# Causal attention on Trainium2: TensorE takes scores and values of two sets in turn, where it took one and one

## What is computed

```python
# second attention (called AG in the kernel): softmax, causal, 16 heads of 8
scores = jnp.einsum('bhqd,bhkd->bhqk', q, k) / np.sqrt(HD)
probs = jax.nn.softmax(jnp.where(causal, scores, -1e30), axis=-1)
out = jnp.einsum('bhqk,bhkd->bhqd', probs, v)
# last attention (AR): relu, causal, 16 heads of 8
att = jax.nn.relu(scores) * causal
att = att / (jnp.sum(att, axis=-1, keepdims=True) + 1e-09)
ctx = jnp.einsum('bhqk,bhkd->bhqd', att, v)
```

## Time and profile before

| | |
|---|---|
| median of 3 runs | 1069.61 us (1068.16 to 1070.17) |
| the profiled execution's own time | 1072.35 us |
| its span in the trace | 1070.2 us |
| mean granted TensorE clock | 0.937 of full speed |
| TensorE busy with matmuls | 959.2 us, 90% |
| VectorE, ScalarE, GpSimd busy | 543.8, 544.1, 148.1 us |

### The profile page before, as it was taken

One profiled execution on the slowest core, in us unless ns is written; L12 is line 12 of the kernel. 1 busy time (PEld: TensorE's weight loads), 2 busy tenths in 40 slices (PEclk: granted clock), 3 DMA queues, 4 the chain that ended last, 5 costly groups with the idle time before them and its releaser, 6 DMA issues.

```text
span 1070.2 us, 24001 instructions
## 1 busy us (share of the span) xinstructions
PE 959.2 (90%) x10552; PEld 444.5 (42%) x10552; DVE 543.8 (51%) x878; ACT 544.1 (51%) x767; POOL 148.1 (14%) x164
## 2 busy tenths in 40 slices
PE   7357878899999998997899798998999999999898
PEld 3245653333333334884333333443333333344343
DVE  4535544553333356565555444546666665424454
ACT  5114444589999965542745551227555554445121
POOL 2300110050100103101011040000223223004000
PEclk9689998999999999558999899999999999998999
DMA  9564310010000000000000017400000000000841
GB/s 306 159 148 103 95 45 2 0 41 2 2 2 2 2 2 1 4 4 2 0 1 0 1 39 155 113 14 0 2 2 2 2 2 2 0 1 32 162 111 54
DMA packets 18851, 43.23 MB, mean 40 GB/s; under 512 B 5360, under 2 KB 5808, under 8 KB 17200
## 3 DMA queue, kind: packets, MB, share of 16 engines
q1 hardware_dynamic: 18748, 41.71, 15.3%
HBM read 36.91 MB, written 4.55 MB: 39 GB/s over the span
## 4 chain that ended last, share of the span: by engine, by line
PE 72%; ACT 8%; DVE 8%; DMA 7%; SPq 3%; issue 2%; POOL 0%; DVEq 0%; POOLq 0%
PE ps L1588 72%; DMA stf<-aux 2%; ACT nrr L798 2%; ACT nrr L796 1%; DMA stf<-scr_w 1%; SPq L516 1%; SPq L591 1%; DVE mxq L1215 1%; ACT work L1043 1%; DMA scr_k<-work 1%; DMA scr_q<-work 1%; DMA hz<-aux 0%; DVE work L1542 0%; ACT nrr L785 0%; SPq L560 0%
## 5 line engine op out<-in xcount | busy, mean ns | idle before, releaser
L1588 PE MATMUL ps<-rq,stf 32*64 32x512 f32 (+4 forms) x4096 | 213.4, 469 | 3.0 <-ACT hz L946 1.6
L1588 PE MATMUL ps<-work,vbuf 64*32 64x96 f32 (+6 forms) x3712 | 197.0, 387 | 0.7 <-issue 0.5
L1588 PE MATMUL ps<-hz,wsb 128*128 128x512 f32 (+1 forms) x352 | 161.3, 620 | 4.0 <-ACT nsq L787 3.5
L1588 PEld LDWEIGHTS ps<-rq,stf 32*64 32x64 f32 x4096 | 102.3, 152 | 108.0 <-issue 80.3
L902 ACT ACTIVATE work<-ps 128x1024 f32<-128x1024 f32 x144 | 139.3, 1022 | 13.5 <-PE ps L1588 8.8
L1588 PEld LDWEIGHTS ps<-work,vbuf 64*32 64x32 f32 (+1 forms) x3712 | 72.8, 121 | 110.3 <-issue 63.0
L964 ACT ACTIVATE work<-ps 128x1024 f32<-128x1024 f32 x72 | 73.7, 1025 | 75.6 <-PE ps L1588 75.6
L1588 PE MATMUL ps<-work,wsb 128*128 128x512 f32 (+1 forms) x176 | 90.8, 610 | 10.6 <-DVE work L1495 7.8
L1588 PEld LDWEIGHTS ps<-hz,wsb 128*128 128x128 f32 (+1 forms) x352 | 62.2, 191 | 83.7 <-issue 70.3
L1012 ACT ACTIVATE work<-ps 128x512 f32<-128x512 f32 x48 | 28.7, 597 | 124.9 <-PE ps L1588 124.9
L1291 DVE TENSOR_TENSOR work<-work,csb 128x1024 f32<-128x1024 f32 (+1 forms) x40 | 41.6, 1040 | 95.9 <-ACT work L902 95.6
(11 more groups left out here) (195 smaller groups left out, 1182.1 us busy)
## 6 DMA issues: line engine op xcount, KB each, us to landing
stf<-scr_w SPq DMA_DIRECT2D x128, 128.0 KB, 4.0
wsb<-in_w SPq DMA_DIRECT2D x1, 3440.0 KB, 19.9
stf<-scr_q SPq DMA_DIRECT2D x12, 192.0 KB
rq<-in_rq SPq DMA_DIRECT2D x2, 1024.0 KB, 5.1
csb<-in_c SPq DMA_DIRECT2D x1, 2003.0 KB, 11.8
stf<-scr_k SPq DMA_DIRECT2D x9, 204.0 KB
scr_q<-work SPq DMA_DIRECT2D x6, 256.0 KB, 5.3
scr_k<-work SPq DMA_DIRECT2D x6, 256.0 KB, 5.4
```

The costliest lines, as they stand in the source:

```text
L1588: return nc.tensor.matmul(o, l, r, start=start, stop=stop, skip_group_check=True)
```

## The change

The order of the four calls on TensorE in `causal_attention` changes, for AG and AR. Nothing is added or removed: the matmuls, the waits inside `scores` and `values`, the buffers and the programs of the other engines are the same.

```diff
-                for n in range(NS * len(PASSES) + 2):
-                    if n < NS * len(PASSES):
-                        scores(n)
-                    if n >= 2:
-                        values(n - 2)
-                    if n == NS * len(PASSES):
-                        denominators(a, 0)
+                for n in range(0, NS * len(PASSES), 2):
+                    for ahead in (n, n + 1):
+                        scores(ahead)
+                    if n:
+                        for behind in (n - 2, n - 1):
+                            values(behind)
+                values(NS * len(PASSES) - 2)
+                denominators(a, 0)
+                values(NS * len(PASSES) - 1)
```

## The result

The changed kernel takes 1136.4 us (median of 4, 1132.3 to 1139.7) against 1069.9 for the kernel before in the same comparison: a ratio of 1.061, 95% interval 1.0555 to 1.0664, or 59 to 71 us slower. A second comparison with more runs gave 1134.0 (6 runs) against 1070.8 (11 runs), ratio 1.0585 (1.0544 to 1.0626), 58 to 67 us. The forecast was 1130.6 with a range of 1121 to 1146; the forecast difference of 61 us lies in both intervals.

A forecast was written before the change was run, and what follows sets the result against it. TensorE was taken to bound AG and AR; 0.89 us more a round, with start and tail, gave about +30.5 us in each, +61 on 1069.6, so 1130.6 us, range 1121 to 1146.

The forecast's parts named there:

- The ring: Each AG and AR round: first unit's reading, release, fourth unit, two values, next first unit: 5.14 us against 4.25.
- the fourth unit: Last score unit in a round of two sets; needs the first unit's PSUM banks, may start 2.2 us after it.
- the blocked unit: In TensorE's list, the last score unit of a round, awaiting its PSUM banks; values and all that follows wait behind it.
- the first rival: AG and AR: banks free in time, TensorE saves 0.25 us in each of 72 rounds, 1052 us; chance 0.05.
- The covers: Other waits in AG and AR (ScalarE's and VectorE's readings, `probs`, masks) fit within the 5.14 us round and add nothing.
- First and last round: In AG, first round 3.6 us, last readings 2.2 us, and a tail about 1.5 us longer from VectorE's late mask.
- the sum: AG from first Exp to last: 3.6 + 174.8 + 2.2 = 180.6 us; both attentions together +61 us.
- The rival with a falling clock: AG and AR: TensorE stands still about 1.2 us in each 5.14, so its clock falls; likelier 1147 us; chance 0.07.
- A change of kind: TensorE switching between scores and values in AG and AR: some 0.09 us each over going on with the same kind.

The follow-up runs named there:

- half Exp: ScalarE's Exp in AG over one head of each unit: changed kernel, AG from 187.0 to 170.4 us; kernel before, AG from 156.8 to 150.6.
- moved fourth unit: Changed kernel with the second unit of scores n + 1 issued after one set of values: 1124.8 us, ratio 1.0497.
- with the waits away: AG alone in twos, six one-bank PSUM places, both heads summed in one 64-row matmul: AG 138.5 us, against 148.8 in the old order.

## Why the prediction was right

**The ring.** It was forecast at 5.14 us and is 5.11. Reading 1.02 and release 0.05 came as read from the earlier trace rows; the fourth unit to the values 1.02 against 1.01 to 1.03; the start of scores to their reading 1.15 against 1.16. Values were put at 1.90 and took 1.85. The half Exp showed that the reading is on the ring once, and the moved fourth unit that the wait hangs on its place. In 36 of 36 rounds of AG and 35 of 36 of AR the fourth unit starts 0.05 us after the reading of the first ends.

**Who waits behind it.** Nothing passed the blocked unit from the third round on in either stage (the values start 1.02 us after it, rounds of 5.11 us throughout), and the first rival (1052) fell. The rule of the Trainium skill, "TensorE: Matmul & The Clock Gate" (Part 3, Packing small matmuls), that matmuls keep the order of the program, agrees with the trace so far as the wait goes. It doesn't agree within a set, where the odd unit's first passes start before the even unit's second ones.

**The covers.** The masks, the ring of `probs` and VectorE's units in AR cost nothing in the middle, as said: AG and AR have the same round to the hundredth, though their readers differ.

**First and last round.** From the first Exp to the last in AG 180.1 us were measured (229.4 to 409.5) against 180.6 by the sum. Two errors stand against each other in it: the ring too long by 0.03 us makes 1.1 us in 34 rounds, and in the last round the Exp of the fourth unit follows 2.75 us behind that of the first, not 2.2, since ScalarE reads the second and third unit in between. At the end the wait for VectorE's late mask is there, at its place:

```profile
410.02 0.69 DVE L1278 COPY nrr<-ps 128x512 f32<-128x512 f32 x1 [5.14 <-PE ps L1588]
410.63 1.82 DVE L1291 TENSOR_TENSOR work<-work,csb 128x512 f32<-128x512 f32 x2
...
411.46 1.06 PE L1588 MATMUL ps<-work,vbuf 128*32 128x512 f32 x8 [0.65 <-DVE work L1291]
```

The copy of the bank, the mask behind it, and TensorE's 0.65 us of idle time before the values of set 70. AG grew by 30.2 us and AR by 29.7, against 30.5 each: AR's values have no such wait at the end, and its sum was 0.8 us too high.

**The clock.** The rival with a falling clock fell: 1.00 in AR and 0.99 in AG as before. Its premise was too strong. Of the 1.2 us that TensorE was to stand still in each round, the third unit fills all but some 0.45 us, and the records show TensorE busy for 177.4 of 187.4 us in AG.

**Where the reasoning was off.** One reading and one size, neither of which the 61 us hung on.

The wait was said to cost nothing in the kernel before, and TensorE's work to be the whole of its 4.25 us. But the odd unit waited for ScalarE there too, in both attentions, and 0.14 us of each old round of AG hung on that reading. The 0.07 by which the odd unit is behind the even one was read as TensorE's own and is this wait. It stood in the numbers: the fourth unit "over 2 us" after the first, the release 2.2 us after it. The difference of 5.14 and 4.25 doesn't change by it, since 4.25 is measured.

A change of kind was put at 0.09 us and costs 0.15. I had compared the gap between kinds with the pass right behind a change, 0.45, and not with passes of one kind, 0.43. So the saving is 0.30 us a round and not 0.25; its share on the ring is why two sets of values took 1.85 and not 1.90. With both errors the first rival's gain was too small: with the waits away AG took 138.5 us in twos against 156.8 before, though that kernel leaves out half of the exponentials and adds up scores that belong apart.

The 61 us were of the right size within the stages (59.9). The ratios of the two comparisons come to 65 and 63 us, 2 to 4 above 61, with 61 inside both intervals; that excess, open as said above, is no part of the sum.

## What to carry to other kernels

Before units of one kind are grouped, count the buffers that stand between producer and consumer: four units in a row through three places put a producer behind a reader of its own group, and everything that follows in the producer's list waits as well. The price can be read from the kernel before: add up the ring (read, release, last unit, what stands behind it, first unit until it can be read) and set it against the present round. A grouping that saves 0.30 us a round is worth having only with enough places that this ring stays shorter than the round. And before a wait is called free, compare the start of the waiting work with the end of what it waits for: here they were 0.05 us apart in the kernel before, which busy shares don't show.

## What the runs showed that I had not expected

With one head of 32 rows a unit, in the old order, the whole of AG ran at 1.2 GHz (granted clock 0.50) though its records show TensorE busy for 272.73 of 272.80 us. The low level had begun at 230.0, before AG's first scores at 231.7, and lasted until 503, with the last scores done and the last values running. With 64 rows a unit and the same number of columns, the clock was low for the first 5.5 us of AG, up to 236.4, and at 1.00 from then on:

```profile
236.40:379.70 143.30, 143.30 (x1524) 40.86 (x1528) 50.77 (x55) 76.48 (x141) 7.49 (x4) 1.00 0.01 2
```

A full busy share by the records thus didn't tell here whether the clock would rise. In the order of twos the same half-empty matmuls had 1.00 from 239.2 on. These are single profiles, and what decides between the two was not tried.
